# The order of work in a decoder layer: query transfers by halves, a norm in ScalarE for three groups, and all steps in a new order

## What is computed

```python
x = _layernorm(x + attn(x))          # linear attention: exp features of q and k, 16 heads
x = _layernorm(x + xattn(x, ctx))    # softmax attention, 16 heads of 8, keys and values from ctx
x = _layernorm(x + ffn(x))           # ternary 128->512, gelu, layernorm over 512, ternary 512->128
```

## Time and profile before

| | |
|---|---|
| median of 3 runs | 639.41 us (639.32 to 640.41) |
| the profiled execution's own time | 637.62 us |
| its span, first to last instruction | 635.5 us |
| PE busy | 598.7 us (94%) |
| POOL, DVE, ACT busy | 479.4, 495.4, 451.3 us |
| mean granted clock of PE | 0.976 |
| wait of score for the packed queries | 17.5 us, 16 times |

### The profile page before, as it was taken

How to read it: one execution, slowest core, us unless ns; L and a number is a source line. 1 busy time by engine, 2 the same in 40 slices (tenths; PEclk the granted TensorE clock), 3 DMA queues, 4 the chain that set the end, 5 groups by cost and what they waited for, 6 DMA issues and landing times.

```text
span 635.5 us, 31020 instructions
## 1 busy us (share of the span) xinstructions
PE 598.7 (94%) x13344; PEld 440.7 (69%) x13344; DVE 495.4 (78%) x1279; ACT 451.3 (71%) x831; POOL 479.4 (75%) x619
## 2 busy tenths in 40 slices
PE   9999999999999999999999999999999999985784
PEld 6786777677676767767677767767676777674664
DVE  2655677877787888878788887888787888879787
ACT  4546566968777795978778795968778696957642
POOL 5425054988889798888889888888979888898744
PEclk9999999999999999999999999999999999998578
DMA  8103224164544537165545636275533825344500
GB/s 341 56 24 105 77 70 87 45 157 57 155 92 102 112 94 152 46 153 86 129 86 119 129 79 150 54 161 86 124 90 113 135 70 122 76 109 87 102 18 33
DMA packets 116153, 64.87 MB, mean 102 GB/s; under 512 B 94321, under 2 KB 100850, under 8 KB 115890
## 3 DMA queue, kind: packets, MB, share of 16 engines
q1 hardware_dynamic: 116018, 62.91, 42.6%
HBM read 17.27 MB, written 4.19 MB: 34 GB/s over the span
## 4 chain that ended last, share of the span: by engine, by line
PE 65%; ACT 10%; SPq 8%; DMA 7%; DVE 4%; issue 4%; POOL 2%; POOLq 0%; DVEq 0%; ACTq 0%
PE bank L337 14%; PE bank L357 9%; PE bank L327 8%; SPq L1298 8%; DMA pack<-Ql 5%; ACT qT L577 4%; PE bank L449 3%; PE bank L414 3%; PE bank L318 3%; PE bank L435 2%; ACT PT L665 2%; ACT Qh L626 2%; PE bank L492 2%; PE bank L295 2%; PE bank L512 2%
## 5 line engine op out<-in xcount | busy, mean ns | idle before, releaser
L337 PE MATMUL bank<-Mh,GT 128*32 128x128 f32 x4096 | 128.3, 274 | 0.1
L337 PEld LDWEIGHTS bank<-Mh,GT 128*32 128x32 f32 x4096 | 107.1, 110 | 21.0 <-issue 17.8
L918 DVE TENSOR_REDUCE mx<-bank 128x8 f32<-128x512 f32 x128 | 79.1, 683 | 29.0 <-PE bank L414 28.9
L665 ACT ACTIVATE PT<-bank 128x512 f32<-128x512 f32 x128 | 64.4, 628 | 33.6 <-PE bank L435 33.6
L550 ACT ACTIVATE Cb<-bank 128x512 f32<-128x512 f32 x81 | 48.4, 598 | 42.8 <-PE bank L337 38.5
L327 PE MATMUL bank<-kp,xs 64*128 64x512 f32 x256 | 76.2, 626 | 0.0
L1191 POOL TENSOR_TENSOR gall<-gall,lnr 128x512 f32<-128x512 f32 x56 | 72.9, 1313 | 1.4 <-DVE st L853 1.4
L550 ACT ACTIVATE GT<-bank 128x512 f32<-128x512 f32 x95 | 50.5, 601 | 28.8 <-PE bank L327 26.2
L1196 POOL TENSOR_TENSOR gs<-gall,gs 128x512 f16<-128x512 f32 x56 | 64.0, 1161 | 8.4 <-ACT gs L702 8.4
L1135 POOL TENSOR_TENSOR rstd<-ve,mhalf 128x4 f32<-128x4 f32 x60 | 63.7, 1061 | 5.0
L598 ACT ACTIVATE x<-x,nmr,rstd 128x128 f32<-128x128 f32 x120 | 50.1, 512 | 19.2 <-POOL nmr L1150 19.2
(11 more groups left out here) (203 smaller groups left out, 1564.2 us busy)
## 6 DMA issues: line engine op xcount, KB each, us to landing
pack<-Qh SPq DMA_DIRECT2D x64, 128.0 KB, 2.7
xT<-in_xT SPq DMA_DIRECT2D x16, 256.0 KB, 3.6
xs<-in_x_nat SPq DMA_DIRECT2D x16, 256.0 KB, 2.6
cxT<-in_cxT SPq DMA_DIRECT2D x16, 256.0 KB, 3.0
Kp<-Kh SPq DMA_DIRECT2D x32, 128.0 KB, 2.1
pack<-Ql SPq DMA_DIRECT2D x32, 128.0 KB, 2.6
out_y<-yo SPq DMA_DIRECT2D x15, 256.0 KB, 2.5
Kp<-Kl SPq DMA_DIRECT2D x16, 128.0 KB, 2.2
```

Of the source, the lines that this page charges most:

```text
L337: m = e.matmul(bk[32 * j:32 * j + 32, tile(g_)], GT[b % 4][:, tile(hh, 32)], Mh[:, tile(hh)], start=True, stop=True)
L665: e.activation(PT[tp][:, tile(j, 512)], bank[uses["prob", s, i][0]][:, :], ACT.Exp, scale=SM).then_inc(emptied("prob", s, i)[0], 1)
L918: e.tensor_reduce(to, bank[uses["score", s, i][0]][:, :].rearrange("p (g b k) -> p g b k", g=2, b=4), AX.X, ALU.max).then_inc(emptied("sco ...
```

## The change

The transfers of Qh wait for each half by itself: the two transfers of half 0 are issued once the first half is written, then the two of half 1. `ap3` can be given to ACT as `ap1` and `ap2` can; for this POOL computes two more small things in `st3` for every group (the negated mean `nm` and its product `nmr` with the root). In `TAIL` `ap3` has the `+` for groups 11, 12 and 14. All three strings are written anew with the same 1325 steps. In `PERIOD`, `qproj@1` stands before `q3`, `vproj` after `proj1@2` and `k3@-1` before `score0@1`, `down2@4` before `q0`, `xb` before `ab1@1`, `stat@3` before `gl0@3`, `loadx@-2` before `kpack`; `x1s` and `ap3` are moved over the end of the period (`ap3@5` and `x1s@1` at its start, on SP the store first), and `split` and `csplit` change places in the same way (`split@-2` last, `csplit` after `x1s@1`).

```diff
--- before.py
+++ after.py
@@ -33,25 +33,25 @@
 
 
 HEAD = """
-zeros wk wq wb split small1 k0 qz k1 csplit k2 g0 WkT WqT mh0 mh1 split@1 g1+ g2+ g3 loadx k3 q0 Wvp xw nbeta c0 small2 ks c1+ kst c2 c3+ g4 g5+ bv
-g6+ loadc g7+ q1 q2 q3 Wff k0@1 gam c4+ dT g0+@1 g1+@1 loadx@1 k1@1 bias2 xb biasA c5 loadx@2 c6+ c7 bc sbar o k2@1 vproj st1 kpack kproj x1s ap1+
-bias3 k3@1 csplit@1 c0+@1 g2+@1 g3@1 loadc@1
+WkT wk wq wb k0 k1 small1 k2 k3 q0 mh0 g0 mh1 g1 g2 xw g3 g4 g5+ WqT q1 zeros loadx c0+ c1+ c2+ ks Wvp small2 c3+ Wff g6+ g7+ kst q2 q3 loadx@1 loadc
+split gam bv csplit c4+ c5+ split@1 c6+ nbeta loadc@1 k0@1 bias2 c7 dT g0+@1 g1@1 k1@1 biasA xb bc qz sbar o g2+@1 g3+@1 st1 k2@1 k3@1 kproj ap1+
+vproj bias3 loadx@2 c0@1 kpack split@2
 """
 PERIOD = """
-split@-1 g4 g5 gs0@3 qpack@1 q0 ab2@3 c1 ks pv0@2 gs1@3 up0@3 down2@4 down3@4 up1@3 gs2@3 kpack cs0@2 up2@3 up3@3 gl0@3 gl1@3 kst stat@3 c2+ c3
-oturn0@2 pv1@2 q1 q2 q3 qproj@1 c4 gh0@3 gh1@3 loadx@-2 c5+ loadc@-1 dT cs1@2 ab1@1 g6+ g7+ oturn1@2 kproj k0@-1 vproj proj0@2 gs3@3 k1@-1 k2@-1
-score0@1 c6+ c7+ score1@1 g0+@-1 g1+@-1 xb g2+@-1 g3+@-1 proj1@2 st2@2 gh2@3 k3@-1 rows@1 down0@3 gl2@3 down1@3 gh3@3 gl3@3 bc ap2+@2 c0+@-1 st3@4 o
-st1 csplit@-1 prob0@1 prob1@1 x1s ap3@4 ap1+
+ap3@5 g4 g5 x1s@1 csplit down2@4 q0 c1 ab2@3 gs0@3 ks pv0@2 up0@3 gs1@3 gs2@3 up1@3 kst cs0@2 qpack@1 down3@4 up2@3 stat@3 gl0@3 up3@3 c2+ gl1@3 c3
+pv1@2 q1 q2 oturn0@2 qproj@1 q3 gh0@3 c4+ c5 dT gh1@3 oturn1@2 cs1@2 g6+ g7+ k0@-1 xb proj0@2 k1@-1 kproj k2@-1 k3@-1 score0@1 loadx@-2 c6+ ab1@1 c7+
+score1@1 gs3@3 g0+@-1 g1+@-1 g2+@-1 g3+@-1 gh2@3 kpack proj1@2 st2@2 vproj rows@1 loadc@-1 gh3@3 down0@3 gl2@3 gl3@3 ap2+@2 down1@3 bc c0+@-1 st3@4 o
+st1 prob0@1 prob1@1 ap1+ split@-2
 """
 TAIL = """
-g4@1 qpack@2 q0@1 ab2@4 kpack@1 down2@5 c1@1 pv0@3 ab1@2 ks@1 oturn0@3 up0@4 up1@4 kst@1 tw@1 gs0@4 down3@5 cs0@3 c2+@1 up2@4 up3@4 stat@4 q1@1 gs1@4
-pv1@3 qproj@2 kproj@1 g5+@1 gl0@4 gh0@4 g6+@1 gs2@4 q2@1 oturn1@3 cs1@3 proj0@3 q3@1 gl1@4 c3+@1 dT@1 g7+@1 score0@2 gh1@4 score1@2 xb@1 c4+@1 c5+@1
-gs3@4 c6+@1 proj1@3 c7+@1 rows@2 gh2@4 st2@3 gl2@4 gl3@4 gh3@4 bc@1 ap2+@3 o@1 st1h0@1 prob0@2 down0@4 prob1@2 ap1h0+@1 st1h1@1 st3@5 down1@4 down2@4
-ap1h1+@1 pv0@2 ab2@3 oturn0@2 qpack@1 pv1@2 gs0@3 gs1@3 down3@4 up0@3 oturn1@2 flip+@1 stat@3 gl0@3 up1@3 up2@3 up3@3 gs2@3 qproj@1 vproj@1 ap3@5
-proj0@2 proj1@2 gh0@3 gh1@3 gl1@3 st2@2 gs3@3 score0@1 gh2@3 score1@1 down0@3 ap2+@2 rows@1 gh3@3 gl2@3 ab1@1 st3@4 gl3@3 flip3@2 down1@3 prob0@1
-ap3@4 prob1@1 down2@3 pv0@1 oturn0@1 pv1@1 ab2@2 down3@3 oturn1@1 up0@2 up1@2 proj0@1 up2@2 turn0+@2 turn1+@2 st2h0@1 ap2h0+@1 st3@3 up3@2 proj1@1
-st2h1@1 stat@2 flip3h0@1 turn2+@2 turn3@2 ap2h1+@1 ap3@3 flip3h1@1 up0@1 down0@2 down1@2 down2@2 up1@1 down3@2 up2@1 turn0+@1 up3@1 turn1+@1 st3@2
-ab2h0@1 ab2h1@1 stath0@1 stath1@1 turn2+@1 down0@1 ap3@2 turn3+@1 down1@1 down2@1 st3h0@1 down3@1 st3h1@1 ap3h0@1 ap3h1@1
+ap3@6 g4@1 down2@5 csplit@1 x1s@2 q0@1 qpack@2 xb@1 gs0@4 cs0@3 up0@4 pv0@3 down3@5 oturn0@3 c1+@1 gs1@4 tw@1 ks@1 ab2@4 up1@4 up2@4 up3@4 stat@4
+gh0@4 kproj@1 kpack@1 gl0@4 pv1@3 c2@1 qproj@2 q1@1 g5+@1 g6+@1 proj0@3 q2@1 q3@1 kst@1 c3@1 cs1@3 oturn1@3 gs2@4 c4+@1 c5+@1 c6@1 gh1@4 ab1@2
+score0@2 gl1@4 dT@1 gl2@4 score1@2 gs3@4 proj1@3 gh2@4 g7+@1 c7+@1 rows@2 st2@3 gl3@4 gh3@4 bc@1 o@1 ap2+@3 st1h0@1 prob0@2 prob1@2 st1h1@1 ab2@3
+qpack@1 ap1h0+@1 st3@5 gs0@3 pv0@2 down0@4 down1@4 gs1@3 gl0@3 gl1@3 down2@4 up0@3 ap1h1@1 down3@4 flip+@1 up1@3 up2@3 oturn0@2 up3@3 stat@3 qproj@1
+gh0@3 pv1@2 oturn1@2 proj0@2 proj1@2 st2@2 gh1@3 ap3+@5 vproj@1 ap2+@2 score0@1 score1@1 gh2@3 down0@3 flip3@2 rows@1 gh3@3 gs2@3 gs3@3 up0@2 down1@3
+gl2@3 ab1@1 gl3@3 st3@4 prob0@1 ab2@2 prob1@1 turn0@2 down2@3 pv0@1 oturn0@1 down3@3 pv1@1 proj0@1 oturn1@1 st2h0@1 up1@2 ap3+@4 turn1+@2 proj1@1
+st2h1@1 st3@3 up2@2 turn2+@2 stat@2 ab2h0@1 up3@2 ap2h0+@1 ap2h1+@1 flip3h0@1 ap3@3 flip3h1@1 down0@2 turn3+@2 down1@2 down2@2 up0@1 down3@2 turn0+@1
+st3@2 stath0@1 stath1@1 up1@1 up2@1 turn1+@1 down0@1 turn2+@1 up3@1 ap3+@2 down1@1 down2@1 ab2h1@1 st3h0@1 turn3+@1 down3@1 st3h1@1 ap3h0@1 ap3h1@1
 """
 
 
@@ -154,7 +154,7 @@
         gT = [gTs[:, 1024 * t:1024 * t + 1024] for t in range(4)]
         gT32, tpw = [v.bitcast(F32) for v in gT], xT
         st, mv, ve, rstd = [{k: sb(n + k, c) for k in "1234"} for n, c in (("st", 24), ("mv", 8), ("ve", 4), ("rstd", 4))]
-        nm, nmr = [{k: sb(n + k, 4) for k in "12"} for n in ("nm", "nmr")]
+        nm, nmr = [{k: sb(n + k, 4) for k in "123"} for n in ("nm", "nmr")]
         V3 = [v[:, :].rearrange("p (n c) -> p n c", c=32) for v in Vblk]
 
         s_small1, s_WkT, s_WqT, s_Wvp, s_small2, s_Wff, s_bv = [sem(n + "_loaded") for n in ("small1", "WkT", "WqT", "Wvp", "small2", "Wff", "bv")]
@@ -181,7 +181,7 @@
         s_gs, s_gh, s_gl, s_gT = sem("g_scaled"), sem("g_hi"), sem("g_lo"), [sem(f"g{t}_transposed") for t in range(4)]
         by_head = "p (g n) -> p g n"
         s_st, s_mv, s_ve, s_rstd, s_ln = [{k: sem(f"ln{k}_{n}") for k in "1234"} for n in ("stats", "mean", "var_eps", "rstd", "done")]
-        s_nm, s_nmr = [{k: sem(f"ln{k}_{n}") for k in "12"} for n in ("minus_mean", "shift")]
+        s_nm, s_nmr = [{k: sem(f"ln{k}_{n}") for k in "123"} for n in ("minus_mean", "shift")]
 
         ZEROS = 6
         Kown = KSz[:, :].rearrange("p (u r) -> p u r", u=8)[:, :, 0:128].rearrange("p u (t c) -> p u t c", t=4)[:, :, :, 0:4]
@@ -724,10 +724,10 @@
                     {"k": kexp, "q": qexp, "prob": prob, "up": up, "gh": ghi}[name](s, t)
                 elif on_act and name == "flip":
                     flip(s)
-                elif on_act and name in ("ap1", "ap2"):
-                    apply(name[2], s, {"ap1": x1, "ap2": x2}[name][s % 2])
-                elif on_act and name in ("ap1h", "ap2h"):
-                    apply_half(name[2], s, t, {"ap1h": x1, "ap2h": x2}[name][s % 2])
+                elif on_act and name in ("ap1", "ap2", "ap3"):
+                    apply(name[2], s, {"ap1": x1, "ap2": x2, "ap3": yo}[name][s % 2])
+                elif on_act and name in ("ap1h", "ap2h", "ap3h"):
+                    apply_half(name[2], s, t, {"ap1h": x1, "ap2h": x2, "ap3h": yo}[name][s % 2])
                 elif name == "flip3h":
                     flip3_half(s, t)
                 elif on_act:
@@ -1104,9 +1104,6 @@
 
             def st_half(k, s, h):
                 w.wait_ge(s_ln[k], 4 * s)
-                if k == "3":
-                    root_half(k, s, h)
-                    return
                 two_ = slice(2 * h, 2 * h + 2)
                 w.wait_ge(s_mv[k], 4 * s + 2 * h + 2)
                 w.wait_ge(s_nmr[k], s)
@@ -1137,9 +1134,6 @@
             def st(k, s):
                 if s > 0:
                     w.wait_ge(s_ln[k], 4 * s)
-                if k == "3":
-                    root(k, s)
-                    return
                 w.wait_ge(s_mv[k], 4 * s + 4)
                 if s > 0:
                     w.wait_ge(s_nmr[k], s)
@@ -1290,12 +1284,13 @@
                 w.wait_ge(s_qz, 4)
                 if s > 1:
                     w.wait_ge(*filled("prob", s - 2, 7))
-                w.wait_ge(s_qh, 2 * s + 2)
-                for r, src in ((0, Qh), (2, Qh), (1, Ql)):
-                    if r == 1:
-                        w.wait_ge(*emptied("qproj", s))
-                    for i in two:
-                        e.dma_start(Qp[p][4 * i + r:128:8, :], src[64 * i:64 * i + 64, :]).then_inc(s_qp[p], 16)
+                for i in two:
+                    w.wait_ge(s_qh, 2 * s + 1 + i)
+                    for r in (0, 2):
+                        e.dma_start(Qp[p][4 * i + r:128:8, :], Qh[64 * i:64 * i + 64, :]).then_inc(s_qp[p], 16)
+                w.wait_ge(*emptied("qproj", s))
+                for i in two:
+                    e.dma_start(Qp[p][4 * i + 1:128:8, :], Ql[64 * i:64 * i + 64, :]).then_inc(s_qp[p], 16)
 
             def kpack(s):
                 p = s % 2
```

## The result

The kernel takes 629.85 us (median; 628.36 to 631.31) against 639.37 before, a ratio of 0.985 [0.9825, 0.9876]: 9.5 us less, where 13.4 (639.4 to 626) were forecast. The profiled execution took 631.23 us, its span is 629.4.

What follows compares the result with a forecast made beforehand. PE, busy 94% of the span, was taken to set the pace. The terms -9.2 - 2.3 + 0.45 - 2.2 = -13.25 took 637.6 to 624.4 us, given as a median of 626 us, range 619 to 636.

Steps and rivals of the forecast that it cites:

- Eleven waits, -9.2 us: Periods between 140 and 540 us: the last Ql lands 1.35 us earlier, so all eleven score waits go, -9.2 us.
- Three other waits and n = 2, -1.85 together: Score waits of n = 1, n = 3 and the end's start go, -2.3 us; n = 2 waits longer for x1's transpose, +0.45.
- dT's cover, down2, POOL, SP: In the periods: dT keeps 0.2 us of cover, down2 at worst 0.5 to spare, POOL about 31.7 us busy; nothing lost.
- `HEAD`, nothing within 1 us: In HEAD: PE's work and the awaited loads stay the same, so nothing, plus or minus 1 us.
- `TAIL`, -2.2 us: In TAIL, where group 15's chain rules: -2.2 us in sum, called rough, bounds -6 and +3.
- Maxima earlier, -1.5: In TAIL: group 15's maxima start earlier with ap3 on ACT, Qh by halves and half of ap1 on DVE, -1.5 us.
- -1.3 and -1.1: In TAIL: POOL's root for group 13 leaves the last second norm, -1.3 us; group 14's last ap3 leaves DVE, -1.1.
- (b): Rival in the periods: same-side transfers queue, Ql lands only 0.66 us earlier, 2.8 us of waits stay, 629 us; chance 0.13.
- (c): Rival in the periods: the wait moves to dT as q3's exp ends later, 4 us, 630 to 634 us; chance 0.12.
- (d): Slower rival in the periods: down2 waits for a late gT2, about 645 us if 3.1 us late; chance 0.06.
- (e): Rival: no gain, since the transfers, not Qh's time, set the landing; 638 to 640 us; chance 0.03.
- (f): Rival: the end gains all of its waits as well, or g5's gap closes; 615 to 620 us; chance 0.06.

Runs made afterwards that it cites:

- The runs with plain copies: Three kernels with plain copies in place of the 85 DMA transposes: two edit the changed kernel's TAIL (626.53, 624.28 us), one the kernel before, by period (631.15 us).
- The experiment with g7 ahead: Changed kernel with plain copies for its DMA transposes, and g7+@1, c7+@1, score1@2 ahead of gh2@4 and gl2@4 in TAIL: 626.53 us, 0.9782 of the kernel before.
- the old string and the halves: Kernel before with plain copies for transposes; Qh by halves and qproj ahead of q3 switched on by period, its end with old order and halves: 631.15 us, 0.9884.

## Why the prediction was right, and where it was wrong

- **The bound.** Right: PE filled the periods, and the gaps that could be won were score's waits for Ql.
- **Eleven waits, -9.2 us.** Right in mechanism and size. Over the eleven periods up to L357 of the last one it took 395.9 us and takes 386.5: -9.4, every period now 35.13 to 35.17. The sizes of the parts held too: the first issue comes 0.71 us earlier by the halves (0.69 forecast). What the sum didn't say is how much of this is reserve. 1.35 us stood against waits of 0.84 on the average; with 0.7 off each of the eleven waits of before, 2.4 of the 9.2 us would be left (an estimate from the rows of score), so either part alone would have brought most of them.
- **Three other waits and n = 2, -1.85 together.** From L357 of `HEAD` (group 0) to that of n = 3 it took 101.3 us and takes 99.9, 1.4 less (the third of the waits, 0.34 us, lies in `TAIL`); of the wait of n = 1, 1.07 us, 0.19 are left; the wait of qproj for x1T is 0.85, as worked out (0.19 + 0.65).
- **dT's cover, down2, POOL, SP.** Right: no wait of dT for qT, down2 0.46 us ahead of q0 without a wait, POOL 31.2 us a period (31.7 forecast).
- **`HEAD`, nothing within 1 us.** 1.05 us was lost in the filler matmuls, the same 25 with nothing to wait for. The runs with plain copies show 4.62, 5.26 and 5.51 us there, the 5.26 with the old `HEAD`, so the length does not go with the order of `HEAD`; what sets it stays open.
- **`TAIL`, -2.2 us.** This is the step that failed: +4.1 in the profiled execution, over the 3 us at which the prediction called itself wrong. The sum looked at the chain of group 15 and took the stretch before it as given. What was overlooked is ACT's queue: with g7 and c7 given to ACT behind gh2@4, whatever holds gh2 holds PE. POOL's gl0@4 now stands behind tw, ab2 and stat, and the transpose was issued right behind it, so that it landed 1.4 us after PE had run out of other work (554.55), with gh2 and g7's read-out on ACT still to come. The experiment with g7 ahead takes this out, the wait and the slow clock behind it: 5.5 of the 7.3 us of this stretch, and so the 4.1 of the end. The other 1.8 us of the stretch stay in both kernels that have g7 ahead (32.8 instead of 31.0); the sum had this stretch at nothing.
- **The terms of `TAIL` one by one.** "Maxima earlier, -1.5" was wrong even with g7 mended: score of group 15 comes 50.1 us after the last prob of `PERIOD` (48.4 before, 47.7 with the old string and the halves). Its wait of 5.79 us for Ql is gone, but in front of it PE now waits 3.72 us for cT (3.85 with g7 mended, and 1.25 and 1.28 for x2T). What was to come behind prob of group 15, -1.3 and -1.1, did: 36.3 us from there to the end (629.4 - 593.13) against 38.1 before (635.5 - 597.45), and 36.0 with g7 ahead. That the total of the two fits the -2.2 says nothing on each: what `ap3` on ACT brings by itself was not measured.

The rivals. (b), transfers on one side queue: refuted by the landings above. The Trainium skill's rule (SBUF — State Buffer, Door 1: The DMA port swizzle) that partitions 0 to 63 reach only eight of the sixteen ports does not show here: at 128 KB an issue and 0.6 us between issues, the same-side pairs landed in 2.6 us at the median like the others, so the measurement decides against a loss from it in this kernel. (c) and (d), a wait of dT or of down2: neither appeared. (e) is refuted by the 9.4 us of the periods. (f), the end gains all: the wait of score(15) did vanish, but not the time. The slower rival's kind of mechanism, a late gT, did come, in a place that no case had: not in the periods under PE's down2 but in `TAIL` under ACT's gh2.

The median lies 3.9 us over the forecast and the profiled execution 6.8 us over the sum (631.2 against 624.4). Of these 6.8, 6.3 are `TAIL` and 1.05 the filler; the rest nearly cancels. The four executions fall into two pairs, 628.4 and 631.3 us (granted clock 0.980 and 0.986, against 0.974 twice). The one profiled is of the longer pair, while the profiled execution of the kernel before is its shortest (637.62 of 637.62 to 640.41). So the 4.1 us are the loss of this execution; by the medians the whole gains 9.5 us and not 6.4, and how much of the 3.1 us between them lies in the end is not known. That the shorter pair kept the clock behind c7's wait would fit its 2.9 us (the slow stretch costs 0.86 for L337, 0.92 for L318 and 1.69 for L357), but no profile shows it, and it stays open.

## What to carry to other kernels

When steps are dealt anew to engines that work in order, check for each step that PE waits for what stands ahead of it in its engine's queue and what that one in turn waits for: here one read-out behind one cast that waited for a DMA cost 5.5 us in the profiled execution, more than the 2.2 that the new end was to win. Cost the stretch before the critical chain too, not just the chain. And where a wait of about 1 us is attacked by two edits of 0.7 us each, try them one by one: either took most of the waits, and the second the rest, up to 0.6 us a period.

## What the runs showed of the hardware that was not expected

- In a wait of 2.76 us on PE the clock fell to half (1.00 until 555 us, 0.50 from 556), and it came back only at some 566 us: L337 1.94 us instead of 1.08, L318 2.09 instead of 1.17, L357 5.40 instead of 3.71 (its last part at 1.00 again). After a wait of 0.84 us at the same place it stayed at 1.00 and L357 took 3.71. The clock costs 3.5 us there (0.86 + 0.92 + 1.69), more than the wait. Only one execution of each was profiled.
- The 25 filler matmuls at the very start took 4.36, 5.41, 4.62, 5.26 and 5.51 us in five executions, with the same instructions, at a granted clock of 1.00 in the two that were cut out as windows (4.36 and 5.41).
- In the old order one of SP's issues of the packed queries took up to 1.9 us instead of 0.6; issued half by half, none of the 32 of Qh did in one kernel, but one of Ql took 1.5. In the changed kernel itself the longest was 1.6 of Qh and 2.1 of Ql. What makes an issue long stays open.
